# Holding back the loads of the next expert in a mixture-of-experts stage, and one wait fewer at the end

## The chip, the cores and the metric

The kernel runs on one core of a Trainium2 chip. The metric is device time in microseconds (us): the median of several executions. One further execution was recorded by the hardware profiler, and all rows below come from it. The engines are TensorE (PE, with its weight loads as PEld), VectorE (DVE), ScalarE (ACT), GpSimd (POOL) and Sync (SP), which here only issues DMAs.

## What is computed

Sixteen sequences of 256 tokens with 128 features pass through a windowed attention with 16 heads, and then through a layer of 8 experts, of which each token uses 2. The part that matters here is the layer of experts, cut from the reference:

```python
k_probs, k_idx = jax.lax.top_k(softmax(xf @ router_w.T), 2)     # two experts for each token
buf = zeros((E, capacity, H)).at[flat_e, slot].add(dispatched)    # rows queued by expert
h = silu(einsum('ech,ehf->ecf', buf, w1))                         # 128 -> 512
out_buf = einsum('ecf,efh->ech', h, w2)                           # 512 -> 128
combined = sum(out_buf[flat_e, slot] * k_probs[..., None])        # back to the token's row
return combined.reshape(B, T, H) + x
```

E is 8, H is 128, the hidden width is 512, and all numbers are float32.

## The kernel before

The first 340 us of the span are attention and routing. There GpSimd adds each token's row into a queue of its expert in DRAM by indirect DMAs (line 1332). The change leaves that stage alone. The rest of the span is the stage of experts, which loops over e = 0 to 7. The 1284 rows used of an expert are cut into three chunks c of 512, 512 and 260 columns. Every engine runs through the same (e, c) in an order that is written out by hand, and the engines are kept in step by semaphores alone. Nothing is reordered by a scheduler.

Sync loads, in body2(e), first the weights of expert e + 1 (load_weights, lines 443 and 444: w1raw and w2raw, 256 KB each) and then its rows (load_expert, lines 429 and 430: xs, 650 KB). Before, the weights waited only until expert e's weights had been split by ScalarE and those of e - 1 by VectorE. There are two buffers of each.

ScalarE runs, in body2(e), for each chunk four pairs of SiLU (lines 889 and 893) and the splits of transposed rows (line 854). After chunk c it copies out the results of the chunk before. After chunk 0 it also splits the weights of expert e + 1 into two parts of lower precision (split_weights, lines 861 and 862). That step begins with `act.wait_ge(S["w_in"], 32 * e + 32)` for the expert whose weights are split, that is, it waits for the loads. Everything of chunk 1 stands behind it on ScalarE.

VectorE runs, in body2(e), for each chunk four subtractions hidp (line 1287), and then weighs results into ys (weigh_results, line 1229). These results belong to an earlier chunk: after chunk 0 the chunk 1 of expert e - 1, after chunk 1 the chunk 2 of expert e - 1, after chunk 2 the chunk 0 of expert e. After chunk 0 it also makes the second part of the weights of expert e + 1 (lines 1186 and 1188), which waits for ScalarE's. Each chunk c has one buffer ys[c] for all experts, so ys of (e, c) waits until the scatters of (e - 1, c) have landed (semaphore added0, added1 or added2).

TensorE runs, in body2(e), for each chunk: hidden (12 matmuls of xTp and w1p), the transposes of the next chunk's rows (rows_across, line 694), out_of_hidden (12 matmuls of hidp and w2p) of the chunk before, and the transposes of the results of the chunk before that (results_across, line 725).

GpSimd scatters the results: 10 indirect DMAs for each expert (line 1408), 4 for chunk 0, 4 for chunk 1 and 2 for chunk 2, each of which adds 128 rows into `out`. A token's row can be added to by two experts, and so at the start of every expert GpSimd waits until all scatters of the expert before have landed (added_all, line 1405). After the last expert it scatters the few left-over rows (line 1414).

Of the kernel before, what the change touches and what calls it, by code (L numbers as in the profile page):

```python
# [85 lines left out]
def build(nc, x, ctx_in, weights, col_bias, row_bias, consts, consts16, q_rows, k_rows, w1, w2, out):  # L86
# [7 lines left out]
    def tiles_of(c):  # L94

        return [(4 * c + t, t * P, min(P, CHUNKS[c] - t * P)) for t in range(-(-CHUNKS[c] // P))]

    def full_tiles(c):

        return [t for t in tiles_of(c) if t[2] == P]  # L100

    es = ExitStack()
    with es:
# [106 lines left out]
        S = {}  # L210
# [33 lines left out]
        def apart(eng, name):  # L244


            eng.sem_inc(S[name], 1)
# [38 lines left out]
        def _(sp):  # L286
# [126 lines left out]
            def load_expert(e, par):  # L413
                if isinstance(e, int) and e >= EXPERTS:
                    return


                if not isinstance(e, int) or e >= 2:
                    sp.wait_ge(S["tags_s"], (e - 1) * 2)
                    apart(sp, "past_sp")  # L420
                chunk_done(sp, "xt2_mm", 1, e - 1, 0)
                apart(sp, "past_sp")
                start = e * QUEUE
                full = queues[bass.ds(start, 10 * P), :].rearrange("(p t) c -> p t c", t=10)
                if isinstance(e, int) and e == 0:
                    sp.dma_start(xs[par][:, 0:4, :], full[:, 0:4, :]).then_inc(S["xs_first"], 16)
                    sp.dma_start(xs[par][:, 4:10, :], full[:, 4:10, :]).then_inc(S["xs_rest"], 16)
                else:
                    sp.dma_start(xs[par][:, 0:10, :], full).then_inc(S["xs_in"], 16)
                sp.dma_start(xs[par][0:USED - 10 * P, 10, :],  # L430
                             queues[bass.ds(start + 10 * P, USED - 10 * P), :]
                             ).then_inc(S["xs_rest" if isinstance(e, int) and e == 0 else "xs_in"], 16)

            def load_weights(e, par):
                if isinstance(e, int) and e >= EXPERTS:
                    return
                if not isinstance(e, int) or e >= 2:
                    sp.wait_ge(S["w_lo"], (e - 1) * 2)
                    apart(sp, "past_sp")
                if not isinstance(e, int) or e >= 1:  # L440
                    sp.wait_ge(S["w_hi"], e * 2)
                    apart(sp, "past_sp")
                sp.dma_start(w1raw[par][:], w1[e, :, :]).then_inc(S["w_in"], 16)
                sp.dma_start(w2raw[par][:], w2[e, :, :].rearrange("(c f) h -> f c h", f=P)).then_inc(S["w_in"], 16)
# [8 lines left out]
                             ).then_inc(S["left_in"], 16)  # L453

            def body2(e, par):
                load_weights(e + 1, 1 - par)
                load_expert(e + 1, 1 - par)
            experts(sp, body2)
            sp.wait_ge(S["init_out"], 16 * EXPERTS)
            sp.wait_ge(S["dump_out"], 16)  # L460
# [849 lines left out]
        def _(pool):  # L1310
# [86 lines left out]
            def body2(e, par):  # L1397

                for c in range(NCH):
# [7 lines left out]
                    for t, col, n in full_tiles(c):  # L1407
# [5 lines left out]
            pool.wait_ge(S["left_ready"], 1)  # L1413
            g.indirect_dma_start(out, bass.IndirectOffsetOnAxis(ap=left_index[:, 0:1], axis=0),
                                 left_ys[:, 1, :], None, compute_op=ALU.add).then_inc(S["left_added"], 16)
            pool.wait_ge(S["left_added"], 16)


# ---- launch: one core; the host lays weights out and makes constants of the shapes
# [68 lines left out]
```

## Time and profile before

| | |
|---|---|
| median of 3 runs | 539.28 us (537.68 to 541.11) |
| the profiled execution | 543.95 us, of which the span of the trace is 542.2 us |
| share of the span: PE, DVE, ACT, POOL | 76%, 63%, 48%, 61% |
| stage of experts | from about 340 us to the end, 202 us |

The shares are averages over two stages. For this change only the second stage counts. A time in a row below is in us from the start of the span, and a duration beside it is that of one instruction or of a merged piece. A row of line 1408 is one scatter. The first scatters of the eight experts start at 362.88, 385.45, 408.58, 429.51, 450.35, 471.25, 492.73 and 513.57.

### The profile page before, as it was taken

Reading aid. Unit: us, or ns where it says so; the run is one execution under the profiler, and the core shown is the slowest. Engines: PE = TensorE matmul, PEld = TensorE weight load, DVE = VectorE, ACT = ScalarE, POOL = GpSimd, SP = SyncE. Lnnn points to the kernel's source line nnn. Section 1 sums busy time; section 2 is a strip of 40 time slices with the busy share of each in tenths; the row PEclk is TensorE's granted clock in tenths of the full one; section 3 lists DMA queues with packets and bytes.
Section 4 is the critical chain, followed back from the end, with each engine's and each line's share of the span. In section 5 each row is a group of like instructions: output and inputs, shape, how many; then the busy total and the mean of one; then the engine's idle time right before and its main releaser. Section 6 shows DMA issues by size and latency. Waiting matters only on the chain.

```text
span 542.2 us, 16107 instructions
## 1 busy us (share of the span) xinstructions
PE 410.0 (76%) x5587; PEld 317.9 (59%) x5587; DVE 342.5 (63%) x1062; ACT 262.9 (48%) x587; POOL 331.6 (61%) x282
## 2 busy tenths in 40 slices
PE   3362798988989999999989747799997988885100
PEld 2241566766767777776767533488886766674000
DVE  4784376878788888898877542278764635734200
ACT  1110355554665555655545511488987676663000
POOL 7442033377767777777765687028677686686683
PEclk9766798999999999999999966899999899999555
DMA  8997787588887877879895335436464554333331
GB/s 185 227 223 153 203 219 173 158 175 182 195 189 169 175 165 180 184 178 179 172 182 96 43 39 79 138 95 121 66 123 75 95 100 81 29 36 29 29 34 16
DMA packets 89045, 70.31 MB, mean 130 GB/s; under 512 B 8992, under 2 KB 75808, under 8 KB 88480
## 3 DMA queue, kind: packets, MB, share of 16 engines
q1 hardware_dynamic: 68208, 60.09, 43.4%
q0 software_dynamic: 20784, 9.53, 19.6%
q8 instruction: 31, 0.51, 0.4%
q14 instruction: 22, 0.18, 0.1%
HBM read 38.85 MB, written 30.74 MB: 128 GB/s over the span
## 4 chain that ended last, share of the span: by engine, by line
POOL 29%; issue 13%; DMA 8%; PE 3%; SPq 1%; DVE 1%; ACT 1%; POOLq 0%; DVEq 0%
POOL out L1408 20%; POOL queues L1332 7%; DMA out<-ys,row_token 5%; PE bank L470 3%; POOL base L1364 1%; DMA k_scratch<-parts 1%; DMA xres<-in_x 1%; DMA queues<-rows,index 1%; DMA xs<-queues 1%; POOL qk L1378 0%; POOL parts L1384 0%; POOL rest L1381 0%; DVE xTp L1179 0%; PE bank L694 0%; ACT xTp L854 0%
## 5 line engine op out<-in xcount | busy, mean ns | idle before, releaser
L1408 POOL DMA_INDIRECT out<-ys,row_token x80 | 125.1, 1564 | 69.0 <-issue 47.2
L918 DVE TENSOR_REDUCE maxima<-bank 128x4 f32<-128x512 f32 x128 | 87.2, 685 | 49.6 <-PE bank L470 45.4
L1332 POOL DMA_INDIRECT queues<-rows,index x64 | 100.3, 1567 | 19.4 <-issue 19.4
L781 ACT ACTIVATE probs<-bank 128x512 f32<-128x512 f32 x128 | 76.4, 597 | 65.3 <-PE bank L470 61.5
L470 PE MATMUL bank<-xTp,w1p 128*128 128x512 f32 (+1 forms) x288 | 64.8, 376 | 11.3 <-DVE xTp L1179 11.2
L470 PE MATMUL bank<-k_pack,q_pack 128*64 128x128 bf16 x1024 | 55.2, 232 | 20.5 <-DMA k_pack<-k_scratch 17.9
L470 PE MATMUL bank<-hidp,w2p 128*128 128x512 f32 (+1 forms) x288 | 62.2, 364 | 0.0
L470 PE MATMUL bank<-q_pack,k_pack 128*128 128x64 bf16 x1024 | 53.3, 196 | 11.4 <-DMA q_pack<-maxT 10.3
L1287 DVE TENSOR_TENSOR hidp<-hid,hidp 128x512 fp32r<-128x512 f32 (+1 forms) x96 | 55.3, 600 | 10.2 <-ACT hidp L893 9.1
L470 PEld LDWEIGHTS bank<-xTp,w1p 128*128 128x128 f32 x288 | 49.1, 196 | 21.5 <-DVE xTp L1179 13.7
L889 ACT ACTIVATE hid<-bank 128x512 f32<-128x512 f32 (+1 forms) x96 | 52.9, 551 | 17.6 <-PE bank L470 17.3
L470 PE MATMUL bank<-probs,v_sb 128*32 128x64 f32 x2048 | 56.7, 227 | 5.7 <-ACT csb L788 3.2
L893 ACT ACTIVATE hidp<-bank 128x512 fp32r<-128x512 f32 (+1 forms) x96 | 53.3, 555 | 0.0
L1229 DVE TENSOR_TENSOR ys<-bank,row_gate 128x512 f32<-128x512 f32 (+1 forms) x24 | 14.4, 600 | 60.3 <-DMA out<-ys,row_token 59.2
L470 PEld LDWEIGHTS bank<-q_pack,k_pack 128*128 128x128 bf16 x1024 | 37.8, 99 | 24.4 <-DMA q_pack<-maxT 10.2
L470 PEld LDWEIGHTS bank<-k_pack,q_pack 128*64 128x64 bf16 x1024 | 34.4, 113 | 29.3 <-issue 10.8
L470 PEld LDWEIGHTS bank<-hidp,w2p 128*128 128x128 f32 x288 | 46.9, 188 | 7.2
L1378 POOL TENSOR_TENSOR qk<-straight,turned 128x512 f32<-128x512 f32 x16 | 22.3, 1393 | 41.9 <-DVE turned L1022 25.4
L470 PEld LDWEIGHTS bank<-probs,v_sb 128*32 128x32 f32 x2048 | 35.7, 110 | 18.8 <-issue 11.4
L470 PE MATMUL bank<-xcT,wts 128*128 128x256 f32 x128 | 40.3, 447 | 7.2 <-ACT xcT L812 5.6
L1370 POOL TENSOR_TENSOR rstd<-var,half_neg 128x2 f32<-128x2 f32 x16 | 16.6, 1037 | 28.3 <-DVE var L955 28.2
L470 PEld LDWEIGHTS bank<-xcT,wts 128*128 128x128 f32 x128 | 25.0, 215 | 13.3 <-issue 6.3
(138 smaller groups left out, 681.5 us busy)
## 6 DMA issues: line engine op xcount, KB each, us to landing
k_pack<-k_scratch SPq DMA_DIRECT2D x64, 192.0 KB, 3.9
q_pack<-q_scratch SPq DMA_DIRECT2D x64, 128.0 KB, 3.2
queues<-empty SPq DMA_DIRECT2D x8, 682.5 KB, 7.5
xs<-queues SPq DMA_DIRECT2D x7, 650.0 KB
q_scratch<-parts SPq DMA_DIRECT2D x16, 192.0 KB
k_scratch<-parts SPq DMA_DIRECT2D x16, 192.0 KB
xin<-in_x SPq DMA_DIRECT2D x16, 128.0 KB, 3.1
cin<-in_ctx SPq DMA_DIRECT2D x16, 128.0 KB, 3.3
```

The lines of the kernel that those rows point to most:

```text
L470: return nc.tensor.matmul(o, l, r, start=start, stop=stop)
L781: nc.scalar.activation(probs[u % 2][:], bb[u % 2][:], ACT.Exp).then_inc(S["prob_s"], 1)
L889: nc.scalar.activation(hid[s][:, f, 0:CHUNKS[c]], up[f][:, 0:CHUNKS[c]], ACT.Silu).then_inc(S["silu_s"], 1)
L893: nc.scalar.activation(hidp[s][:, 0, f, 0:CHUNKS[c]], up[f][:, 0:CHUNKS[c]], ACT.Silu).then_inc(S["h_hi"], 1)
L918: v.reduce_max(maxima[par][:, 4 * hg:4 * hg + 4, i2], ab[u % 2][:].rearrange("p (h c) -> p h c", c=P), AX).then_inc(S["max_s"], 1)
L1229: v.tensor_tensor(ys[c][:, 0:m, :], yt[:, 0:m * DIM].rearrange("p (t c) -> p t c", c=DIM), row_gate[par][:, t0:t0 + m].unsqueeze(2).to_bro ...
L1287: v.tensor_tensor(hidp[s][:, 1, f, 0:CHUNKS[c]], hid[s][:, f, 0:CHUNKS[c]], hidp[s][:, 0, f, 0:CHUNKS[c]].bitcast(F32), ALU.subtract).then ...
L1332: g.indirect_dma_start(queues, bass.IndirectOffsetOnAxis(ap=index[par][:, n:n + 1], axis=0), rows[par][:, n // TILES, n % TILES, :], None, ...
L1364: g.tensor_tensor(base[par][:], x1[par][:], rows[par][:, 0, :, 0:DIM], ALU.add).then_inc(S["base_s"], 1)
L1370: g.tensor_tensor(rstd1[:], var1[:], half_neg[:], ALU.pow).then_inc(S["rstd1_s"], 1)
L1378: g.tensor_tensor(qk[:], straight[:], turned[:], ALU.add).then_inc(S["qk_s"], 1)
L1408: g.indirect_dma_start(out, bass.IndirectOffsetOnAxis(ap=row_token[par][0:n, t:t + 1], axis=0), ys[c][0:n, col // P, :], None, compute_op= ...
```

## The change

Two waits are edited, and no instruction that does work is added, removed or moved on any engine. Sync now waits, before it loads the weights and rows of expert e + 1, until the four scatters of chunk 0 of experts 0 to e - 1 have landed. And GpSimd no longer waits for the landing of the scatter of left-over rows. Sync has a wait on the same semaphore, `left_added`, at the end of its program, as before.

```diff
             def body2(e, par):
+                if e >= 1:
+                    sp.wait_ge(S["added0"], e * (16 * len(full_tiles(0))))
                 load_weights(e + 1, 1 - par)
                 load_expert(e + 1, 1 - par)
             experts(sp, body2)
@@
             g.indirect_dma_start(out, bass.IndirectOffsetOnAxis(ap=left_index[:, 0:1], axis=0),
                                  left_ys[:, 1, :], None, compute_op=ALU.add).then_inc(S["left_added"], 16)
-            pool.wait_ge(S["left_added"], 16)
```

## Rows read from the trace of the kernel before

**Rows 1.** The page, part 4: the chain that ended last, by engine and line
```profile
POOL 29%; issue 13%; DMA 8%; PE 3%; SPq 1%; DVE 1%; ACT 1%; POOLq 0%; DVEq 0%
```

**Rows 2.** Timeline of GpSimd: start, duration, line, [idle before <-releaser]
```profile
336.11 1.54 POOL L1332 DMA_INDIRECT queues<-rows,index  x1 [0.30 <-issue]
...
362.88 1.53 POOL L1408 DMA_INDIRECT out<-ys,row_token  x1 [25.23 <-issue]
...
368.52 1.82 POOL L1408 DMA_INDIRECT out<-ys,row_token  x1 [0.30 <-issue]
...
379.93 1.54 POOL L1408 DMA_INDIRECT out<-ys,row_token  x1 [0.31 <-issue]
385.45 1.54 POOL L1408 DMA_INDIRECT out<-ys,row_token  x1 [3.98 <-DMA out<-ys,row_token]
...
450.35 1.64 POOL L1408 DMA_INDIRECT out<-ys,row_token  x1 [2.58 <-DMA out<-ys,row_token]
...
467.08 1.54 POOL L1408 DMA_INDIRECT out<-ys,row_token  x1 [0.30 <-issue]
471.25 1.57 POOL L1408 DMA_INDIRECT out<-ys,row_token  x1 [2.64 <-DMA out<-ys,row_token]
...
476.83 1.54 POOL L1408 DMA_INDIRECT out<-ys,row_token  x1 [0.30 <-issue]
...
492.73 1.55 POOL L1408 DMA_INDIRECT out<-ys,row_token  x1 [3.24 <-DVE row_gate L1218]
...
534.42 1.35 POOL L1414 DMA_INDIRECT out<-left_ys,left_index  x1 [2.68 <-DMA out<-ys,row_token]
```

**Rows 3.** Timeline of Sync's DMA issues: start, duration, line
```profile
328.95 0.47 SPq L443 DMA_DIRECT2D w1raw<-in_w  x1
...
339.50 0.34 SPq L426 DMA_DIRECT2D xs<-queues  x1
...
343.52 0.37 SPq L443 DMA_DIRECT2D w1raw<-in_w  x1
...
353.51 0.34 SPq L443 DMA_DIRECT2D w1raw<-in_w  x1
```

**Rows 4.** Timeline of ScalarE: the first split of weights, and the third and fourth
```profile
332.53 0.62 ACT L861 CAST w1p<-w1raw 128x512 fp32r<-128x512 f32 x1 [5.99 <-DMA w2raw<-in_w]
...
368.28 0.69 ACT L861 CAST w1p<-w1raw 128x512 fp32r<-128x512 f32 x1
...
384.79 0.69 ACT L861 CAST w1p<-w1raw 128x512 fp32r<-128x512 f32 x1
```

**Rows 5.** Timeline of VectorE: ys, in the order of the stage
```profile
390.91 0.42 DVE L1229 TENSOR_TENSOR ys<-bank,row_gate 128x256 f32<-128x256 f32 x1
...
407.80 0.42 DVE L1229 TENSOR_TENSOR ys<-bank,row_gate 128x256 f32<-128x256 f32 x1 [0.27 <-DMA out<-ys,row_token]
...
480.16 0.69 DVE L1229 TENSOR_TENSOR ys<-bank,row_gate 128x512 f32<-128x512 f32 x1 [5.47 <-DMA out<-ys,row_token]
...
512.79 0.42 DVE L1229 TENSOR_TENSOR ys<-bank,row_gate 128x256 f32<-128x256 f32 x1 [3.05 <-DMA out<-ys,row_token]
```

**Rows 6.** Timeline of TensorE, 12 matmuls or the transposes of one chunk merged
```profile
394.77 0.60 PE L725 MATMUL bank<-cst,yT 128*128 128x128 f32 x4
...
406.45 0.38 PE L725 MATMUL bank<-cst,yT 128*128 128x128 f32 x2
...
420.32 4.61 PE L470 MATMUL bank<-xTp,w1p 128*128 128x512 f32 x12 [1.08 <-DVE xTp L1179]
...
441.01 3.02 PE L470 MATMUL bank<-xTp,w1p 128*128 128x512 f32 x12 [1.08 <-DVE xTp L1179]
```

**Rows 7.** Stretches: busy us of PE, PEld, DVE, ACT, POOL; then granted clock, DMA share, GB/s
```profile
348.00:350.00 2.00, 1.46 (x7) 0.93 (x6) 0.52 (x1) 0.51 (x2) 0.00 (x0) 0.82 0.26 105
418.00:420.00 2.00, 0.63 (x4) 0.42 (x4) 2.00 (x4) 1.08 (x3) 1.70 (x2) 1.00 0.36 33
420.00:422.00 2.00, 1.68 (x4) 1.40 (x5) 1.46 (x3) 0.06 (x1) 1.69 (x2) 0.60 1.05 187
```

## The prediction

> **What bounds the kernel now.** I read the chain of waits first, then the timeline of each engine in the stage of experts. Of the span, 29% of the chain lies on GpSimd, against 3% on TensorE [rows 1]. For the stage the timeline says more. GpSimd starts a scatter every 1.86 us (5.58 us from 471.25 to 476.83, three steps) and pauses only between experts, where it waits until the expert before has landed: from the last scatter of one expert at 467.08 to the first of the next at 471.25 it is 4.17 us [rows 2]. So a settled expert takes 20.90 us (450.35 to 471.25) [rows 2]. TensorE, ScalarE and VectorE are faster than that and run ahead until the one buffer ys[c] stops them: ys of (6, 0) at 480.16 waited 5.47 us for the scatters of (5, 0), the last of which started at 476.83 [rows 2, 5]. The bound of the stage is GpSimd's row of scatters, and the question is whether the added wait lets any result come later than GpSimd wants it.
>
> Call S the start of an expert's first scatter. S0 is 362.88, S6 is 492.73, and the left-over scatter stands at 534.42 [rows 2].
>
> **What the added wait holds back.** The weights of expert e + 2 (e = 0 to 5, so six loads) now go out after the four scatters of (e, 0) have landed. Before, the weights of expert 2 went out at 353.51 [rows 3]. Now they cannot go before about 372 (fourth scatter of expert 0 at 368.52, plus a landing) [rows 2]. That is 18 us later, and ScalarE split them at 368.28 [rows 4], so they come too late already in the first round.
>
> Queued behind Sync's wait: both weight loads and both loads of rows of that expert, nothing else. Who waits for them: ScalarE's split, in its program after chunk 0 of expert e + 1, and behind the split all of ScalarE's chunk 1, and behind this VectorE's four subtractions of chunk 1 and then ys of (e, 2). This is the place where it bites. GpSimd wants ys of (e, 2) after 8 scatters, 14.8 us after S. It had it long before: ys of (1, 2) stood at 390.91, 5.5 us after S1 at 385.45 [rows 2, 5]. Now it can't exist before chunk 0 of the same expert has been scattered, landed, and answered by a load. The two sides have become one loop, and I add it up from S of one expert to S of the next:
>
> - S to the start of the fourth scatter: 5.58 (471.25 to 476.83) [rows 2].
> - From a last scatter's start to Sync's first DMA that waited for its landing: 3.39 (336.11 to 339.50) [rows 2, 3]. VectorE, which waited for the same kind of landing in the stage of experts, says 3.33 (476.83 to 480.16) [rows 2, 5]. I take 3.4.
> - From the issue of the weights to ScalarE's split that waited for them: 3.58 (328.95 to 332.53), the only load of weights in the trace that an engine stood waiting for, and scatters were under way then too [rows 3, 4].
> - From that split to ys of (e, 2): 6.12 (384.79 to 390.91) [rows 4, 5]. TensorE has done hidden of chunk 1 by then, so the work between is ScalarE's eight SiLUs and VectorE's last subtraction, and I take the row as it stands.
> - From the start of ys of 256 columns to the scatter that it releases: 0.78 (512.79 to 513.57) [rows 2, 5].
> - One further scatter of chunk 2, 1.86, and then landing and start of the next expert, 4.17 (467.08 to 471.25) [rows 2].
>
> The sum is 5.58 + 3.4 + 3.58 + 6.12 + 0.78 + 1.86 + 4.17 = 25.49 us for one expert, where a settled one took 20.90. Cover for the load was only the four scatters of chunk 1.
>
> Of the other things that must be ready, ys of (e + 1, 0) comes out of the same restart: the split stands at S + 12.56, transposes of its results end 10.58 us after a split (384.79 to 394.77 + 0.60) [rows 4, 6], and ys and the issue take about 1.05, so it could be scattered at S + 24.2. That is 1.3 us ahead of 25.49, hence not late, but close. The rows of expert e + 2 go out behind the weights. With weights and rows issued together at 343.52, traffic is down to 105 GB/s in the stretch 348 to 350 [rows 3, 7], so I let them land some 6.5 us after the first issue, about 3 us after the split begins, and TensorE's transposes of them stand behind ScalarE's chunk 1, which is later. They cost nothing.
>
> **What the wait gives back.** The first pause of before was longer than 4.17, 5.52 from 379.93 to 385.45 [rows 2], while it followed a load of rows closely. In the loop such loads go out after chunk 0 and are over before chunk 2 lands, so every pause is 4.17. This gain is in the sum, since I count from S0 to S6 and not by differences: six experts by 25.49 are 152.9 us, and S6 moves from 492.73 to 515.8, which is 23.0 later. The time before for the same six was 129.85.
>
> **The tail.** Nothing is loaded for an expert 8, so ScalarE isn't stopped in expert 7. It is past its last held-back split at S5 + 12.6, and from there to ys of (6, 2) it is 22.7 us in a free run (384.79 to 407.5, where VectorE began to wait for a landing) [rows 4, 5], which is S5 + 35.3 or S6 + 9.8, ahead of the 14.8 of GpSimd's need. From S6 to the left-over scatter it is then 41.7 us, as before (492.73 to 534.42) [rows 2]. Sync's wait in the last round has no load behind it and costs nothing.
>
> **The removed wait.** GpSimd is free at the end of its instruction (534.42 + 1.35) and not after the landing, some 1.3 us earlier. But Sync waits for the same landing, and the program ends when all engines have. I take 0. If the end of the program on GpSimd takes long and was in the way, up to 1.3 us are gained; a loss I exclude, since nothing is added and the landing doesn't depend on who waits.
>
> **Sum.** 23.0 us on the profiled execution, 543.95 to about 567. It stood 4.7 us above the median of the runs, which I take to be a constant of that execution; on the median it is 539.3 + 23.0 = 562.3.
>
> **Rivals.** One, TensorE's clock. The restart finds TensorE idle: in a free run it is done with its share 22.0 us after a split (384.79 to 406.45 + 0.38) [rows 4, 6], and its next work waits for the first SiLUs of the next restart, so every expert has some 5 us of idle before it. The trace shows what this does: in 418 to 420 TensorE was busy 0.63 of 2.00 us, and the granted clock fell from 1.00 there to 0.60 in 420 to 422 (1.00 is 2.4 GHz, and it goes to 1.2), and 12 matmuls took 4.61 us where 3.02 are usual [rows 6, 7]. The Trainium skill ("TensorE: Matmul & The Clock Gate", Part 1: The HAM clock gate) has an idle TensorE fall to half its clock until it has been busy again for a while; the row agrees. In the loop this falls on hidden of chunk 2 and on out_of_hidden of chunk 1 ahead of ys of (e + 1, 0). With 1.6 us more for the latter and 0.3 for transposes it stands at S + 26.1, 0.6 over the loop; if all of it ran at half clock, 3.0 for the 12 matmuls and some 1.2 for the rest, at S + 28.4, 2.9 over. Six times that is 3.6 to 17.4: 566 to 580, and I name 571.
>
> Two, the weights land late because rows are issued right behind them and share the queue: at worst they land with the rows, 6.2 us and not 3.58 after issue, 2.6 by six, 15.7 more: 578. The row of 3.58 had no rows behind it, which speaks for this; that the weights are issued first speaks against it. "DMA: Bandwidth & Descriptors" of the Trainium skill (Anatomy of one DMA) gives 2.0 us and the bytes by 436 GB/s, for a transfer issued by GpSimd, which makes an estimate of 3.2 for the 512 KB; by it the sum would be 2.3 us less, 560.
>
> Three, the other side: the added wait is hidden and only its good part is left, loads that no longer meet landings. The price is the excess of the six experts before over 20.90 each, 129.85 - 125.4 = 4.5: 534.8. It decides if the weights are in before ScalarE reaches the split, or if ys of (e, 2) comes by S + 14.8. By my terms it comes at S + 18.7, and to be hidden the leg from landing to ys, 9.7 us, would have to fit into 5.8. Only a misreading of which expert's load is awaited where could bring that.
>
> Four, no change: the split of expert e + 2 isn't where the order puts it, or the count awaited has always been reached. 538 to 540.
>
> **Chances.** The loop as summed 0.60 (556 to 566: 0.8 us less an expert if landing and loads are at their shortest, 1.3 from the end, 0.6 more if Sync is slower), clock 0.24, late weights 0.06, hidden with a gain 0.04, no change 0.06. The range of 556 to 576 holds the loop and most of the clock's case. Slower by over 1% are the first three, 0.90. The gain of rival three is 0.8%, short of the 1% that a measurement of this kernel can tell from no change, so most of it counts as no change: 0.07, and 0.03 for faster.
>
> **What the profile after would show.** First scatters of experts 0 to 6 about 25.5 us apart, and the last two 20.9. Within each of experts 0 to 5 a hole on GpSimd of about 4.6 us between the eighth and the ninth scatter, released by ys. Before L861 an idle of several us on ScalarE, released by the DMA of w2raw, six times. VectorE's waits for landed scatters, at ys, nearly gone, replaced by waits for ScalarE at L1186 (two lines lower in the new file's numbering is L1188). Weights issued 9 us after S. If the hole stands before the first scatter of an expert and is released by ys of chunk 0, the clock decides. If there is no hole, rival three or four holds. The prediction is wrong if the landing, the load or the restart differ from these single rows in the changed traffic; each 0.5 us there is 3 us in the sum.

## The result, and the profile after

The changed kernel takes 570.08 us (median of 6 runs, 567.18 to 576.25) where the kernel before took 538.34 (6 runs, 537.68 to 541.11). The ratio is 1.0554, with a 95% interval of 1.0516 to 1.0592: 29.8 us slower, by the ratio. It is formed from the runs in the faster of two states that the chip shows, without the one of 576.25, while the two medians as they stand are 31.7 us apart. The forecast was 562.3 in a range of 556 to 576. Direction and mechanism held. The sum said 23.0 us more, and 29.8 were measured.

The profiled execution of the changed kernel took 569.11 us, its span 567.3. The page's part 4 (the chain that ended last, by engine), to be read against [rows 1]:

```profile
POOL 15%; DMA 11%; issue 11%; PE 9%; ACT 5%; DVE 2%; SPq 1%; POOLq 0%; ACTq 0%; DVEq 0%
```

GpSimd's share has halved, and ScalarE, which had 1%, has 5%. The chain now goes through the other engines. These shares are only a hint, as is shown below at one link. The waits in the stage of experts (who waited for what: us in total, times, longest) name the places:

```profile
DVE w1p L1188 <- ACT w2p L864: 52.4, 6, 9.3
ACT w1p L863 <- DMA w2raw<-in_w: 51.7, 6, 9.2
...
DVE ys L1231 <- DMA out<-ys,row_token: 5.7, 2, 3.0
```

Six times ScalarE stands some 8.6 us in front of its split of the weights, VectorE stands behind it, and VectorE's waits for landed scatters are nearly gone. (Line numbers are two higher than before.)

One turn of the loop, expert 2 to expert 3, from the timelines. GpSimd, where the first row is S2 and the last is S3 (start, duration, [idle before <-releaser]):

```profile
411.29 1.54 POOL L1410 DMA_INDIRECT out<-ys,row_token  x1 [2.75 <-DVE ys L1231]
...
417.06 1.54 POOL L1410 DMA_INDIRECT out<-ys,row_token  x1 [0.30 <-DVE ys L1231]
...
424.45 1.54 POOL L1410 DMA_INDIRECT out<-ys,row_token  x1 [0.30 <-issue]
431.88 1.79 POOL L1410 DMA_INDIRECT out<-ys,row_token  x1 [5.89 <-DVE ys L1231]
433.97 1.54 POOL L1410 DMA_INDIRECT out<-ys,row_token  x1 [0.30 <-issue]
438.41 1.54 POOL L1410 DMA_INDIRECT out<-ys,row_token  x1 [2.90 <-DVE ys L1231]
```

Sync's issue, ScalarE's split and VectorE's ys in the same turn:

```profile
420.50 0.34 SPq L443 DMA_DIRECT2D w1raw<-in_w  x1
```

```profile
424.63 0.62 ACT L863 CAST w1p<-w1raw 128x512 fp32r<-128x512 f32 x1 [8.78 <-DMA w2raw<-in_w]
```

```profile
430.66 0.42 DVE L1231 TENSOR_TENSOR ys<-bank,row_gate 128x256 f32<-128x256 f32 x1
...
436.90 0.69 DVE L1231 TENSOR_TENSOR ys<-bank,row_gate 128x512 f32<-128x512 f32 x1 [1.89 <-PE bank L727]
```

Here the loop can be walked: fourth scatter at 417.06, landed, and weights out at 420.50; split at 424.63; ys of (2, 2) at 430.66; the ninth scatter at 431.88, after a hole of 5.89 us; the next expert at 438.41, 27.12 us after the last. Before there was no such hole inside an expert, and an expert took 20.90 [rows 2]. The chain itself takes one link that no wait in the program asks for: it comes to the fourth scatter at 417.06 from a ys, as the row's releaser says too, but that is ys of chunk 1, which the fifth scatter needs. The fourth followed the third after the usual 0.30 us, and the two events merely lie close together. So the loop rests on the timelines and the order of the program, not on the shares. The first scatters stand at 357.56, 384.41, 411.29, 438.41, 464.63, 491.10, 518.45 and 539.92: six turns of 26.8 on the mean, and then one of 21.5, as no load is held back any more.

The tail from the left-over scatter to the end of the span is shorter than before: 560.72 to 567.3 is 6.6 us, where 534.42 to 542.2 was 7.8 [rows 2]. The chain itself doesn't tell the two apart, as it ends in both with GpSimd's work on that scatter, here

```profile
556.54 3.29 DMA out<-ys,row_token
559.97 0.53 issue
560.49 1.57 POOLq L103
```

after the landing of the tenth scatter of expert 7. The gain is read from the two stretches alone.

One thing must be set apart. The first scatter of the stage stood at 362.88 before [rows 2] and at 357.56 after, though nothing in the 340 us ahead of it was changed. In the profiled executions of this study it lies anywhere from 356.4 to 363.5. The stage of experts has to be compared from its own first scatter: 362.88 to 534.42, 171.5 us, before, and 357.56 to 560.72, 203.2 us, after. That is 31.6 more. Less 1.2 at the end it is 30.4, which lies between the 29.8 by the ratio and the 31.7 by the medians.

### The profile page after: what moved, and what is told of

Its sections match the earlier page's. It is cut to its first block, busy times and chain, and to the rows that moved or that the text cites. A ratio compares the mean times of both kernels' runs of the same rounds, so it can differ in the third digit from the quotient of the medians.

```text
span 567.3 us, 16106 instructions
## 1 busy us (share of the span) xinstructions
PE 414.6 (73%) x5587; PEld 326.3 (58%) x5587; DVE 343.2 (60%) x1062; ACT 262.4 (46%) x587; POOL 333.6 (59%) x282
## 4 chain that ended last, share of the span: by engine, by line
POOL 15%; DMA 11%; issue 11%; PE 9%; ACT 5%; DVE 2%; SPq 1%; POOLq 0%; ACTq 0%; DVEq 0%
PE bank L472 8%; POOL out L1410 7%; DMA out<-ys,row_token 6%; POOL queues L1334 6%; DMA w2raw<-in_w 4%; ACT hid L891 2%; ACT hidp L895 2%; PE bank L696 1%; DVE ys L1231 1%; POOL base L1366 1%; DMA queues<-rows,index 1%; DVE xTp L1181 1%; DMA xs<-queues 0%; DVE hidp L1289 0%; ACT xTp L856 0%
## 5 line engine op out<-in xcount | busy, mean ns | idle before, releaser
L1410 POOL DMA_INDIRECT out<-ys,row_token x80 | 127.4, 1593 | 98.3 <-issue 47.7
L472 PE MATMUL bank<-xTp,w1p 128*128 128x512 f32 (+1 forms) x288 | 70.6, 404 | 48.5 <-DVE xTp L1181 48.5
L472 PEld LDWEIGHTS bank<-xTp,w1p 128*128 128x128 f32 x288 | 55.1, 227 | 57.6 <-DVE xTp L1181 50.4
L1289 DVE TENSOR_TENSOR hidp<-hid,hidp 128x512 fp32r<-128x512 f32 (+1 forms) x96 | 57.4, 604 | 25.1 <-ACT hidp L895 23.0
L472 PE MATMUL bank<-hidp,w2p 128*128 128x512 f32 (+1 forms) x288 | 65.5, 378 | 0.0
L472 PEld LDWEIGHTS bank<-hidp,w2p 128*128 128x128 f32 x288 | 49.7, 199 | 8.0
L1380 POOL TENSOR_TENSOR qk<-straight,turned 128x512 f32<-128x512 f32 x16 | 22.3, 1391 | 42.4 <-DVE turned L1024 28.1
L1188 DVE TENSOR_TENSOR w1p<-w1raw,w1p 128x512 fp32r<-128x512 f32 x8 | 5.5, 692 | 59.7 <-ACT w2p L864 59.7
```

Of the source, the lines that this page charges most:

```text
L472: return nc.tensor.matmul(o, l, r, start=start, stop=stop)
L1289: v.tensor_tensor(hidp[s][:, 1, f, 0:CHUNKS[c]], hid[s][:, f, 0:CHUNKS[c]], hidp[s][:, 0, f, 0:CHUNKS[c]].bitcast(F32), ALU.subtract).then ...
L1380: g.tensor_tensor(qk[:], straight[:], turned[:], ALU.add).then_inc(S["qk_s"], 1)
L1410: g.indirect_dma_start(out, bass.IndirectOffsetOnAxis(ap=row_token[par][0:n, t:t + 1], axis=0), ys[c][0:n, col // P, :], None, compute_op= ...
```

## The experiments

The ratios below are against the kernel before on the same chip.

### Only the wait on GpSimd

```diff
 (of the kernel before)
-            pool.wait_ge(S["left_added"], 16)
```

> The kernel before with only GpSimd's last wait removed; the loads are not held back. If the whole slowdown comes from the held-back loads, this gives 537 to 539 us, the same as before within 1%, and the stretch from the left-over scatter to the end of the span keeps its 7.8 us. If GpSimd's end of program is in the way behind its wait, up to 1.3 us are gained. If the removed wait has a part in the slowdown, it shows here as over 540 us.

540.09 us, ratio 0.9966 (0.9927 to 1.0005). The time is a little over the 540 named as a sign of a part in the slowdown, but the kernel before took 540.00 on this chip, so the removed wait has none, and all of the slowdown belongs to Sync's wait. From the left-over scatter at 533.15 to the end of the span at 539.6 it is 6.45 us, 1.3 less than before [rows 2], and it is 6.5 to 6.6 in the changed kernel and in all the experiments that follow. The timing alone can't tell this gain of 0.2% from none, but nine profiles without the wait agree on it against the only one with it. The expected "no change" fits the time, not the profile; the upper bound of 1.3 was the value.

### Rows held back, weights one expert earlier

```diff
+                load_weights(e + 1, 1 - par)
                 if e >= 1:
                     sp.wait_ge(S["added0"], e * (16 * len(full_tiles(0))))
-                load_weights(e + 1, 1 - par)
                 load_expert(e + 1, 1 - par)
```

> The added wait stands between the load of the weights and the load of the rows, so that the rows of expert e + 2 go out as in the changed kernel, and its weights one expert earlier. Theory (the loop runs over weights, ScalarE's split and ys of chunk 2): the loop is open, 537 to 543 us, since rows that land 13 us after S leave time for transposes, 12 matmuls and ys before the next expert. Rival (the late rows stop TensorE, or the mere bunching of loads and scatters costs): 565 us or more.

541.63 us, ratio 1.003 (0.9995 to 1.0066). The theory holds: rows just as late as in the changed kernel cost nearly nothing once the weights are early. But the experts are 21.2 to 21.7 us apart (one 22.6), not 20.9, and the chain points at a second loop, about as long as GpSimd's row of scatters:

```profile
455.99 0.33 SPq L429 DMA_DIRECT2D xs<-queues  x1
456.31 0.04 issue
456.36 4.27 DMA xs<-queues
460.63 0.04 issue
460.67 1.12 PE bank L696 x4
461.79 4.38 PE bank L472 x12
466.17 0.44 PE bank L727 x4
```

Landing of chunk 0, load of rows, their transposes, and then out_of_hidden, which stands behind the transposes in TensorE's program, up to ys of the next chunk 0. It is fed by rows where the first loop is fed by weights. TensorE ran it at a low clock: the granted clock was 0.50 from 459 to 465, and it took 4.38 us for twelve matmuls, where 3.0 is usual [rows 6]. But the loop doesn't decide here. In this turn, the closest one, ys stands at 466.65 and the scatter at 468.19, 1.54 us later, which is the bare time of ys and issue; in the others it is 1.9 to 3.9 us, and five of the six pauses between experts are 4.1 to 4.2 us, as before. What exceeds 20.9 lies in the scatters themselves: from the first to the tenth of an expert it is 17.0 to 17.8 us, where it was 16.7 (450.35 to 467.08 [rows 2]).

### Weights held back, rows one expert earlier

```diff
+                load_expert(e + 1, 1 - par)
                 if e >= 1:
                     sp.wait_ge(S["added0"], e * (16 * len(full_tiles(0))))
                 load_weights(e + 1, 1 - par)
-                load_expert(e + 1, 1 - par)
```

> The added wait stands behind the load of the rows and before the load of the weights, so that the weights of expert e + 2 go out as in the changed kernel and its rows one expert earlier. Theory: nothing is won, 565 to 572 us, at best 0.2 to 0.6 us less for each of six experts because the weights no longer share the queue with rows. Rival (the rows are what comes late): under 550 us.

572.8 us, ratio 1.0597 (1.0534 to 1.066), turns of 26.7 to 27.9 us, just over the 565 to 572 expected. Late weights alone give all of the slowdown. Nothing was won by taking the rows out of the queue: from issue to split it is still 3.6 to 4.1 us, so the rival of the prediction in which weights land late because of rows behind them falls.

### The split moved out of the way

```diff
 ScalarE
-                    if c == 0:
+                    if c == 1:
                         split_weights(e + 1, 1 - par)
 VectorE
-                    if c == 0:
-                        rest_of_weights(e + 1, 1 - par)
                     if c == 1:
                         tags(e, par)
+                        rest_of_weights(e + 1, 1 - par)
```

> The changed kernel, with both waits as it has them, but ScalarE's split of the next weights and VectorE's part of it stand after chunk 1 and not after chunk 0, and so no longer ahead of ys of (e, 2). Theory: the load is as late as before, 9 us after S, but ys of (e, 2) does not wait for it, and the hole between the eighth and ninth scatter is gone; 536 to 543 us. If what costs is the late load itself, or its traffic beside the scatters of chunk 1, the time stays at 560 us or more. If holding back the loads has a gain of its own (no landing meets a load), it shows here as a time under 536.

561.09 us, ratio 1.0377 (1.0327 to 1.0427). A miss. The first loop is open: ys of chunk 2 now stands 3.3 to 3.8 us ahead of the split and 5.6 ahead of its scatter, and the hole inside an expert is gone. Yet the turns are 24.3 to 25.6 us. The pause between experts has grown to 7.0 to 8.1, and the chain says why:

```profile
445.79 0.34 SPq L443
...
446.81 0.38 SPq L429
...
447.24 6.16 DMA xs<-queues
...
453.44 1.11 PE bank L696 x4
454.55 5.10 PE bank L472 x12
459.65 0.44 PE bank L727 x4
```

It is the second loop, over the rows, and here it decides: ys of the next chunk 0 stands the bare 1.5 us ahead of its scatter in five of the six turns. With weights ahead of them the rows are issued 1.0 us later and take 6.2 us to land, against 4.3 alone, and the twelve matmuls behind them take 5.1. So my sentence in the expectation that the late load itself would have to cost was half right: what costs is the late rows behind late weights. Two loops had been closed by one wait, and the longer hid the other.

### Both loops opened

```diff
 Sync, and ScalarE and VectorE as in the experiment before
+                load_expert(e + 1, 1 - par)
                 if e >= 1:
                     sp.wait_ge(S["added0"], e * (16 * len(full_tiles(0))))
                 load_weights(e + 1, 1 - par)
-                load_expert(e + 1, 1 - par)
```

> Only the weights are held back, as in the kernel where that alone gave loops of 27 us, and the split stands after chunk 1. Both loops found so far are open (the one over the weights and ys of chunk 2, and the one over the rows and ys of the next chunk 0): 537 to 543 us, experts 21 to 22 us apart. If a third thing binds, for example the split itself ahead of chunk 2, the experts stay 24 us or more apart.

542.13 us, ratio 1.0031 (0.9989 to 1.0072). The weights are as late as in the changed kernel, and it costs at most 0.7%. Nothing but the place of the split separates this kernel from the one with the weights held back and the rows one expert earlier, which took 572.8 us: so it is the split on the path that turns late weights into lost time. The turns are 21.3 to 22.3 us. GpSimd has no hole left, and the pause is a landing again (the tenth scatter of expert 3, the first of expert 4):

```profile
444.28 1.65 POOL L1409 DMA_INDIRECT out<-ys,row_token  x1 [0.30 <-issue]
448.48 1.54 POOL L1409 DMA_INDIRECT out<-ys,row_token  x1 [2.55 <-DMA out<-ys,row_token]
```

### Rows first, then weights

```diff
 ScalarE and VectorE as above
                 if e >= 1:
                     sp.wait_ge(S["added0"], e * (16 * len(full_tiles(0))))
-                load_weights(e + 1, 1 - par)
                 load_expert(e + 1, 1 - par)
+                load_weights(e + 1, 1 - par)
```

> Rows and weights both held back by the full wait and the split after chunk 1, but the rows are issued first. With weights first, the rows landed 6.2 us after their issue and the experts were 25 us apart; rows that were alone landed after 4.3 us. If the length of the queue ahead of the rows is the cause, the loop shrinks by about 1.0 for the issue and 1.9 for the landing, to 21.5 to 22.5 us, 541 to 548 us in all. If the traffic of both together is the cause whatever the order, it stays at 24 to 25 us, 556 us or more.

548.18 us, ratio 1.0146 (1.007 to 1.0223), turns of 21.5 to 24.1 us, 22.6 on the mean. It is the queue ahead of the rows: issued first, at 441.53, the rows are used at 445.47 (TensorE's timeline), 3.9 us later.

```profile
445.47 0.66 PE L696 MATMUL bank<-cst,xs 128*128 128x128 f32 x4 [2.35 <-DMA xs<-queues]
```

Now the weights wait behind the rows (from issue to split 5.3 to 7.1 us and not 3.6), and this closes a third loop. VectorE makes its part of the weights ahead of chunk 2 and of ys of the next chunk 0, so that this ys stands behind the late split. The turn from expert 2 to expert 3, on ScalarE, VectorE and GpSimd:

```profile
426.22 0.62 ACT L863 CAST w1p<-w1raw 128x512 fp32r<-128x512 f32 x1 [5.54 <-DMA w2raw<-in_w]
```

```profile
427.39 0.69 DVE L1188 TENSOR_TENSOR w1p<-w1raw,w1p 128x512 fp32r<-128x512 f32 x1 [5.85 <-ACT w2p L864]
...
430.56 0.68 DVE L1231 TENSOR_TENSOR ys<-bank,row_gate 128x512 f32<-128x512 f32 x1
```

```profile
432.07 1.54 POOL L1409 DMA_INDIRECT out<-ys,row_token  x1 [3.98 <-DVE ys L1231]
```

From the split to this ys it is 4.34 us in all six turns, and in four of them the ys stands no more than 1.55 us ahead of its scatter, the bare time, so there it decides. The turn shown adds up: 5.54 to the fourth scatter, 3.39 to the rows' issue, 1.10 to the weights', 7.06 to the split, 4.34 to ys and 1.51 to the scatter are 22.94, from 409.13 to 432.07. So both the queue ahead of the rows and the queue ahead of the weights count, and the time and the turns came out just over the ranges I expected.

### TensorE kept busy through the wait

```diff
 (of the changed kernel, TensorE, body2)
                     elif not first:
                         results_across(e - 1, c + 1, s)
+                    if c == 1 and 1 <= e <= 6:
+                        pe.wait_ge(S["left_kept"], e)
+                        for n in range(7):
+                            mm(downs[s][:], wts[:, WO:WO + DIM], wts[:, 0:512])
```

> The changed kernel, with 7 matmuls whose results nobody reads (0.87 us each at full clock) on TensorE in the stretch in which it stands idle before each of the six held-back restarts. Theory of the clock: the granted clock stays at 1.00 through the restart, from the split to ys of the next expert's chunk 0 it is 10.6 us and not 11.1 to 12.3, the loops of the first three experts fall from 26.9 to about 26.3, and the median falls by 1 to 4 us. Rival (the clock is no term of the loop): ys of chunk 0 comes earlier but the loops stay at 26.2 to 27.3.

570.67 us, ratio 1.0597 (1.0545 to 1.0649). The expected fall of the median by 1 to 4 us didn't come. The granted clock was kept at 1.00 through the restart in two of the six turns, the first and the fifth, in which TensorE was idle for 0.65 and 2.41 us ahead of it. In the other four, with 2.2 to 3.5 us of idle, it fell. The stretches after the filler in the fourth turn, in which the split stands at 449.7 (columns as in [rows 7]):

```profile
450.00:452.00 2.00, 1.80 (x5) 0.49 (x3) 1.09 (x2) 2.00 (x5) 1.54 (x1) 1.00 0.96 231
452.00:454.00 2.00, 0.00 (x0) 0.00 (x0) 1.84 (x4) 2.00 (x6) 0.00 (x0) 1.00 0.51 76
454.00:456.00 2.00, 1.98 (x14) 1.98 (x15) 1.52 (x3) 2.00 (x7) 0.00 (x0) 0.87 0.01 2
456.00:458.00 2.00, 2.00 (x8) 1.71 (x7) 1.98 (x11) 1.93 (x7) 1.01 (x1) 0.50 0.00 0
458.00:460.00 2.00, 2.00 (x8) 1.59 (x8) 0.99 (x3) 0.45 (x2) 1.70 (x2) 0.77 0.35 31
```

Reckoned from these shares the clock is low from about 455.5 to 458.9. In the changed kernel's fourth turn, with the split at 451.0, stretches of half a microsecond give 451.7 to 458.5. So with the filler it falls some 5 us later after the split and is low for 3.4 us and not 6.8.

Still the experiment tells the two apart. From the split to ys of the next chunk 0 it is now 9.7 us in the two turns at full clock and 11.2 to 11.3 in the other four, where the changed kernel had 11.1 to 12.3, and that ys stands 2.3 us or more ahead of its scatter in every turn, so it decides nowhere. The turns show it: 26.76 and 26.73 at full clock, 26.43 to 26.75 in the other four. In the changed kernel it stood 1.5 ahead, the bare time of ys and issue, in the second and third turn, at the edge of deciding. A clock that decides would lengthen the pause before the next expert. There these two pauses were 4.29 and 4.44 us, and with the filler they are 4.36 and 4.18. So the clock cost at most some 0.3 us in the third turn and nothing that shows in the others. The mean turn is 26.64 against 26.82, which is 1 us in all, but of the gain in the second and third turn 0.39 us each is the time from the weights' issue to the split (3.88 and 3.74 against 4.27 and 4.13), and no run says why that was shorter.

### The same wait, one expert earlier

```diff
-                if e >= 1:
-                    sp.wait_ge(S["added0"], e * (16 * len(full_tiles(0))))
+                if e >= 2:
+                    sp.wait_ge(S["added0"], (e - 1) * (16 * len(full_tiles(0))))
```

> The added wait asks for one expert less: weights and rows of expert e + 2 go out when chunk 0 of expert e - 1 has landed. Theory: they land 12 us before the next expert starts, no loop is closed, and the time is that of the kernel before less 1.2 us for the removed wait, 536 to 540 us. If loads timed in this way also keep out of the way of landings, the two long pauses of 5.5 us after the first experts go, 3 us more. Rival (any wait of the loads for scatters costs): over 550.

537.81 us, ratio 0.9991 (0.9952 to 1.003). It isn't that loads wait for scatters, but for which. The two long pauses of 5.5 us are gone here: after the first two experts it is 4.27 and 4.23. But one of them was gone in the first experiment as well, in which no load is held back (4.14 and 5.44). The time isn't better for it. Some scatters of chunk 0 of the next expert take longer to issue:

```profile
377.70 1.68 POOL L1410 DMA_INDIRECT out<-ys,row_token  x1 [2.73 <-DMA out<-ys,row_token]
379.69 1.96 POOL L1410 DMA_INDIRECT out<-ys,row_token  x1 [0.30 <-DVE ys L1231]
381.95 1.73 POOL L1410 DMA_INDIRECT out<-ys,row_token  x1 [0.31 <-issue]
383.99 1.94 POOL L1410 DMA_INDIRECT out<-ys,row_token  x1 [0.30 <-issue]
386.23 1.55 POOL L1410 DMA_INDIRECT out<-ys,row_token  x1 [0.30 <-issue]
```

Usual is 1.54. Six experts took 128.9 us from first scatter to first scatter, with the free loads of the first experiment 129.1. It isn't the loads that make these scatters slow. Sync's issues on either side of them are

```profile
369.31 0.33 SPq L429 DMA_DIRECT2D xs<-queues  x1
...
387.84 0.34 SPq L443 DMA_DIRECT2D w1raw<-in_w  x1
```

and from 379 to 385 the DMA engines moved 33 GB/s, the scatters' own traffic, where it was 187 and 231 in stretches with loads under way (420 to 422 in [rows 7], and 450 to 452 with the filler). Over the ten profiled executions, of 208 scatters that started 0.3 to 5.5 us after the issue of a load 25 lasted over 1.60 us, of the other 592 it was 145. What the slow ones have in common is VectorE: 259 scatters ran while no VectorE instruction did, and none of them lasted over 1.56 us; of the 541 that overlapped one, 170 lasted over 1.60 us, up to 2.04. The scatters of chunk 0 run beside VectorE's subtractions. That VectorE's work is the cause fits this, but no run changes it alone.

## Why the prediction was right, and where its size was off

**The bound, the place, the loop.** Right. GpSimd's row of scatters bounds the kernel before; the added wait closes a loop over landing, weights, ScalarE's split, and ys of chunk 2; and the signs that were named are there: six idles on ScalarE before the split, a hole of 5.2 to 6.0 us before the ninth scatter, weights out about 9 us after S, waits for landings replaced at VectorE. That late weights alone do it is shown by a run, and so is that the time returns when the split is moved off the path while the rows stay early.

**The terms.** The turn was 26.8 and not 25.49 us. On the mean of six turns:

| term | forecast | measured |
|---|---|---|
| S to the fourth scatter | 5.58 | 5.78 |
| to Sync's first DMA | 3.4 | 3.51 |
| issue to split | 3.58 | 3.78 |
| split to ys of chunk 2 | 6.12 | 6.03 |
| ys to the ninth scatter | 0.78 | 1.21 |
| ninth to tenth | 1.86 | 2.10 |
| tenth to the next S | 4.17 | 4.42 |

The largest miss is "from the start of ys of 256 columns to the scatter that it releases: 0.78". That row was misread. 512.79 is ys of (7, 2), and the scatter at 513.57 is the first of expert 7, which was released by the landing before it; the profile named ys only because it came last. ys takes 0.42 us, and the first scatter starts 0.79 after its end. The next scatter follows by 2.10, since the ninth lasts 1.79 and not 1.54: it now runs beside VectorE's restart, with which slow scatters go together (see the experiment before). The two together are 0.67 of the 1.3. The way from S to the fourth scatter is longer by 0.20 for the same kind of slow scatters.

**Gain from undisturbed landings.** "Every pause is 4.17" was too bright. It is 4.26 to 4.33 in four turns, 4.44 in the one that the clock stretched most, and 4.88 after expert 5, where it was long before too (4.78, 487.95 to 492.73). Nor is it shown that the load of rows had made the first pause long. In the experiment with free loads the tenth scatter follows the issue of the rows by 4.1 us as well (375.33 to 379.46), and the pause is 4.14 and not 5.52. What made it 5.52 stays open.

**The tail.** From S6 to the left-over scatter 42.3 us, 0.6 more than the 41.7 forecast.

**The removed wait.** "I take 0" was wrong: 1.2 to 1.3 us came, about the upper bound. So something at the end of GpSimd's program stood behind the wait; the profiles show no instruction there, and what it is stays open.

Six turns by 1.33 are 8.0, with 0.6 of the tail and less 1.2 at the end 7.4 more than the 23.0 forecast, 30.4, beside 29.8 measured. All seven terms but one were too small, each by 0.43 us or less, and all count six times.

**The rivals.** The clock fell as described, to 0.50 in every restart, but the loop was longer than the sum, 26.8 us, and ys of the next chunk 0 only reached the edge of deciding: at most some 0.3 us in one turn, where this rival had 0.6 to 2.9 in each of six. "Late weights" falls: 3.5 to 4.3 us from issue to split, where the rival had 6.2. The estimate from the Trainium skill ("DMA: Bandwidth & Descriptors", Anatomy of one DMA) was 3.2, given for a transfer that GpSimd issues, and the 3.78 measured for Sync's two loads decides against it. For the rows I had written "they cost nothing", which is right beside the longer loop and wrong by itself: without that loop they held the turn at 25.0 us (the split moved, both loads late). Their landing ("some 6.5 us after the first issue") was under-sized, 7.6 in the turn shown of that experiment (445.79 to 453.39), and I had put TensorE's next work behind ScalarE's chunk 1 without the matmuls and the low clock after the rows.

No version beat the kernel before beyond the measurement. The removal of GpSimd's last wait is the only part worth keeping, and it is worth 1.2 us by the profiles.

## What to carry to other kernels

When a wait ties a load to progress further down the pipeline, follow the load to who waits for it and on to what stands behind that step in its engine's program; if the path leads back to the wait, it is a loop, and its length is the new period. Look for all such loops: here one wait closed two, opening the longer gave back only 9 of 30 us, and another order of the loads closed a third. And check in the program that what a row or the chain names as releaser really is what the waiting instruction needed, above all where two events lie within a microsecond. For a loop, the test is whether its last step stands the bare time ahead of the instruction that it is said to hold up.

## What the runs showed of the hardware

- A queue of loads delays what is behind it: the 650 KB of rows landed 4.3 us after issue alone, 6.2 behind 512 KB of weights; the weights reached their split 3.5 to 4.3 us after issue when first and 5.3 to 7.1 when behind the rows.
- GpSimd's first indirect DMA after ys begins 1.21 us after ys starts. Over ten profiles, each of the 259 scatters of 128 rows with no VectorE instruction beside it lasted 1.54 to 1.56 us, and of the 541 with one beside it 170 lasted over 1.60, up to 2.04. Loads under way made no such difference (25 of 208 over 1.60, against 145 of 592).
- TensorE, idle for 6.6 to 8.2 us in each turn, had its granted clock at 0.50 (1.2 GHz) before it was needed again, and kept it for the first matmuls. Seven matmuls cut that idle to 0.7 to 3.5 us. The clock then stayed at 1.00 in two of the six turns, and fell later in the other four.
- From the start of GpSimd's last scatter to the end of the span it took 6.5 to 6.6 us in nine profiles without a wait for its landing on GpSimd, and 7.8 in the one with it.
